# VectorE adds the residual and the LoRA output ahead of the transposed q and copies layer 1's k ahead of the row maxima; ScalarE writes layer 1's high pieces

## The chip, the core and the metric

One Trainium2 chip, one of its cores. The metric is the device time of one execution in microseconds (us), the median of three. The profile's engines are PE (TensorE), DVE (VectorE), ACT (ScalarE), POOL (GpSimd) and SP (SyncE, which issues DMAs only).

## What is computed

Two layers of gated cross attention with a feed-forward part behind each, on x of 8 x 128 tokens by 512 and a context of the same shape. Cut to its core, the reference is:

```python
x = x + tanh(g_xattn[0]) * attn0(layernorm(x), ctx)   # 32 heads of 128, 8 kv heads, RMS norm on q and k
x = x + tanh(g_ffn[0])   * lora(layernorm(x))         # 8 experts of rank 16, a softmax router
x = x + tanh(g_xattn[1]) * attn1(layernorm(x), ctx)   # 16 heads of 96, 4 kv heads, no norm
x = x + tanh(g_ffn[1])   * swiglu(layernorm(x))       # 512 -> 1792 -> 512
# attn: kv = [context, latents]; q, k, v = projections; out = softmax(q k^T / sqrt(hd)) v @ Wo
```

All of it is float32. The kernel gets near that accuracy with pairs: a value is written as a high piece (fp32r, as TensorE reads it) and a low piece (the value less the high one), and each product is three matmuls, high by high, high by low and low by high (`mm3`, L467 to L469).

## The kernel before

There is no scheduler: each engine's program is written out by hand, and semaphores join them. A group is one kv head with its four q heads; layer 0 (`L0`, name "a") has 8 groups, layer 1 (`L1`, name "c") has 4. Within a group a loop runs over the 8 batch elements, so there are 64 + 32 = 96 steps of one tile each. Every engine has its own `step(L, g, b)`, and in it three tiles are under way: the values and the output projection of tile b and of the one before (`prev`), the scores and the softmax of the next (`one`), and the k, v and q projections of the one after (`two`).

TensorE's step is `kv_proj(two)`, `scores(one)`, `q_proj(two)`, `k_turn(two)` (transposes k, L536), `values(b)`, `project(prev)`, `q_turn(two)` (transposes q, L546). Around it the other engines do this:

- ScalarE copies PSUM to SBUF with the high rounding (L706), squares q and k for layer 0's RMS norm (L737, L723), and does the exponentials (`exps`, L760).
- VectorE subtracts for the low pieces (L938), takes the row maxima (`row_max`, L1012), copies layer 1's k (`kv_low`, L988), and adds the projected output to x (`y_add`, L1054).
- The probabilities are divided by their sums and split into a high and a low fp16 piece (`split_probs`: L1029, L1031, high L1036, low L1041). SyncE transposes the pieces by DMA (L426), GpSimd casts them to fp32r (`cast_probs`, L1249), and `values` in the next step reads them. `i` is the half: heads 0 and 1, or 2 and 3.

Three stretches have more in a step than that. In layer 0's first group a layer norm (number 0) stands beside the attention. From the third step of layer 0's last group (L0, g 7) into layer 1's first group, a step also carries the layer norm ahead of the LoRA part (`beside_norm`, number 1), the LoRA part of a tile (`lora`) and the layer norm ahead of layer 1 (`second`, number 2): the tiles run through the seam between the layers one behind the other, and TensorE does `lora_project`, `norm_turn` (L493), `lora_turn` (L607) and `lora_project_out` for them. In layer 1's last group the layer norm ahead of the FFN (number 3) stands beside it. A layer norm is `norm_stats` on VectorE (L950, L952), the reciprocal root on GpSimd (L1218), `norm_scale` on VectorE (L960), `norm_turn` on TensorE, and a high and a low piece on ScalarE and VectorE. `lora_scale` (L1069 to L1073) writes the activations that `lora_turn` transposes; `router_logits` (L1061, L1063) feeds the router's exponential on ScalarE; `lora_add` (L1084) puts the result into x.

The last steps of layer 1 also start the FFN's weights: GpSimd issues their DMAs (L1319, L1320, L1298 and later), among its casts. The FFN then runs by itself to the end.

## Time and profile before

| | |
|---|---|
| median of 3 runs | 1400.72 us (1399.91 to 1400.87) |
| the profiled execution | 1396.48 us, span 1394.4 us |
| PE, DVE, ACT, POOL busy | 94%, 74%, 49%, 36% of the span |
| steps 0 to 95 (both layers) | until 1227 us |
| FFN | 1227 to 1394 us |

Busy time is the union of an engine's instructions; matmuls overlap, and their ends are modelled, so a busy PE is one that has no gap. A step is told by where its `kv_proj` starts on PE: an undisturbed one takes 11.84 us in layer 0 and 10.29 us in layer 1. The granted clock is a share of TensorE's full 2.4 GHz; 0.5 is 1.2 GHz.

### The profile page before, as it was taken

Reading aid. Unit: us, or ns where it says so; the run is one execution under the profiler, and the core shown is the slowest. Engines: PE = TensorE matmul, PEld = TensorE weight load, DVE = VectorE, ACT = ScalarE, POOL = GpSimd, SP = SyncE. Lnnn points to the kernel's source line nnn. Section 1 sums busy time; section 2 is a strip of 40 time slices with the busy share of each in tenths; the row PEclk is TensorE's granted clock in tenths of the full one; section 3 lists DMA queues with packets and bytes.
Section 4 is the critical chain, followed back from the end, with each engine's and each line's share of the span. In section 5 each row is a group of like instructions: output and inputs, shape, how many; then the busy total and the mean of one; then the engine's idle time right before and its main releaser. Section 6 shows DMA issues by size and latency. Waiting matters only on the chain.

```text
span 1394.4 us, 24169 instructions
## 1 busy us (share of the span) xinstructions
PE 1312.8 (94%) x7776; PEld 1150.6 (83%) x7776; DVE 1030.9 (74%) x2620; ACT 680.4 (49%) x2354; POOL 508.2 (36%) x808
## 2 busy tenths in 40 slices
PE   7899999999999999999999888899999998579998
PEld 6788888888888888888887777788888888468887
DVE  5688777777787787777778877888888888533433
ACT  5456665555565566556664433355444543222221
POOL 2445544554455355445544423133223332300000
PEclk8999999999999999999999999999999999789999
DMA  6233332332332332323333211242433322740000
GB/s 189 56 82 76 60 85 62 75 91 46 83 82 46 91 76 61 83 60 73 87 62 68 51 31 31 61 88 58 84 65 72 79 46 47 210 136 1 31 0 31
DMA packets 233439, 98.11 MB, mean 70 GB/s; under 512 B 204800, under 2 KB 217600, under 8 KB 233344
## 3 DMA queue, kind: packets, MB, share of 16 engines
q1 hardware_dynamic: 210416, 58.75, 21.7%
q10 hardware_dynamic: 18992, 27.28, 6.5%
q0 software_dynamic: 3936, 11.01, 2.6%
q8 instruction: 35, 0.57, 0.2%
q14 instruction: 60, 0.49, 0.1%
HBM read 39.08 MB, written 2.10 MB: 30 GB/s over the span
## 4 chain that ended last, share of the span: by engine, by line
PE 71%; DVE 17%; ACT 4%; issue 4%; POOL 2%; DMA 2%; DVEq 0%; SPq 0%; POOLq 0%; ACTq 0%
PE bank L467 18%; PE bank L469 18%; PE bank L468 18%; PE bank L692 7%; DVE split L938 5%; PE bank L678 4%; DVE mx L1012 3%; PE bank L546 3%; DMA turned<-pieces 2%; ACT split L706 2%; DVE pieces L1041 1%; PE bank L536 1%; ACT scratch L760 1%; DVE x L1054 1%; DVE scratch L960 1%
## 5 line engine op out<-in xcount | busy, mean ns | idle before, releaser
L467 PE MATMUL bank<-split 128*128 128x256 f32 (+6 forms) x2120 | 716.7, 338 | 15.5 <-issue 7.2
L469 PE MATMUL bank<-split 128*128 128x256 f32 (+6 forms) x2120 | 696.5, 329 | 0.0
L468 PE MATMUL bank<-split 128*128 128x256 f32 (+6 forms) x2120 | 695.9, 328 | 0.0
L467 PEld LDWEIGHTS bank<-split 128*128 128x128 f32 (+2 forms) x2120 | 405.4, 191 | 48.9 <-issue 10.3
L469 PEld LDWEIGHTS bank<-split 128*128 128x128 f32 (+2 forms) x2120 | 404.6, 191 | 36.4 <-issue 0.2
L468 PEld LDWEIGHTS bank<-split 128*128 128x128 f32 (+2 forms) x2120 | 405.9, 191 | 28.2
L706 ACT ACTIVATE split<-bank 128x512 fp32r<-128x512 f32 (+7 forms) x456 | 194.4, 450 | 325.5 <-PE bank L546 264.0
L1249 POOL CAST split<-turned 128x512 fp32r<-128x512 f16 x384 | 227.9, 622 | 333.9 <-DMA turned<-pieces 333.9
L938 DVE TENSOR_TENSOR split<-bank,split 128x512 fp32r<-128x512 f32 (+7 forms) x456 | 228.0, 503 | 144.0 <-ACT split L706 140.1
L1041 DVE SCALAR_TENSOR_TENSOR pieces<-scratch,rs,pieces 128x256 f16<-128x256 f32 x384 | 180.4, 511 | 0.0
L760 ACT ACTIVATE scratch<-bank,nb,rq 128x256 f32<-128x256 f32 x256 | 141.8, 561 | 63.9 <-DVE nb L1017 63.8
L1012 DVE TENSOR_REDUCE mx<-bank 128x2 f32<-128x512 f32 x192 | 132.1, 688 | 53.4 <-PE bank L469 50.5
L1036 DVE TENSOR_SCALAR pieces<-scratch,rs 128x256 f16<-128x256 f32 x384 | 136.7, 398 | 12.6
L1222 POOL TENSOR_TENSOR split<-raw,split 128x512 fp32r<-128x512 f32 (+1 forms) x90 | 112.4, 1261 | 17.5 <-ACT split L706 16.6
L692 PE MATMUL bank<-split 128*128 128x512 f32 x448 | 107.4, 393 | 0.0
L692 PEld LDWEIGHTS bank<-split 128*128 128x128 f32 x448 | 85.3, 191 | 18.0
L760 ACT ACTIVATE scratch<-bank,nb 128x256 f32<-128x256 f32 x128 | 59.2, 473 | 56.9 <-DVE nb L1020 56.9
L1265 POOL TENSOR_TENSOR qvar<-qsum,hd_eps 128x4 f32<-128x4 f32 x64 | 14.2, 222 | 196.6 <-ACT bank L737 196.6
L723 ACT ACTIVATE scratch<-bank 128x128 f32<-128x128 f32 x128 | 34.3, 274 | 98.5 <-PE bank L469 98.5
L1054 DVE SCALAR_TENSOR_TENSOR x<-bank,tg_attn,x 128x512 f32<-128x512 f32 x96 | 71.0, 740 | 7.1 <-PE bank L469 7.1
L737 ACT ACTIVATE bank<-bank 128x128 f32<-128x128 f32 x256 | 71.3, 284 | 0.0
L706 ACT ACTIVATE split<-raw 128x512 fp32r<-128x512 f32 (+2 forms) x118 | 67.4, 610 | 6.2 <-DMA raw<-in_wkv_a 4.8
(69 smaller groups left out, 1135.3 us busy)
## 6 DMA issues: line engine op xcount, KB each, us to landing
raw<-in_wq_a ACTq DMA_DIRECT2D x14, 512.0 KB, 3.6
raw<-in_wo_a ACTq DMA_DIRECT2D x14, 512.0 KB, 3.4
raw<-in_wkv_a ACTq DMA_DIRECT2D x7, 512.0 KB, 3.4
split<-in_gate_t POOLq DMA_DIRECT2D x2, 1792.0 KB, 7.6
split<-in_up_t POOLq DMA_DIRECT2D x2, 1792.0 KB, 11.2
turned<-pieces SPq DMA_TRANSPOSE x192, 3.1
raw<-in_wq_c ACTq DMA_DIRECT2D x8, 384.0 KB, 3.3
split<-in_down_t POOLq DMA_DIRECT2D x1, 2816.0 KB, 10.6
```

The source lines that it names most:

```text
L467: pe.matmul(out, whi, mhi, start=start, stop=False)
L468: pe.matmul(out, whi, mlo, start=False, stop=False)
L469: return pe.matmul(out, wlo, mhi, start=False, stop=stop)
L692: last = pe.matmul(bank[bk + m % 2][:, :], w[:, k, m * P:(m + 1) * P], part[:, k, toks], start=k == 0 and i == 0, stop=k == KC - 1 and i == 1)
L706: return act.activation(out, in_, ACT.Copy)
L760: act.activation(probs[:, h, :], bank[h // 2][:, (h % 2) * KV:(h % 2 + 1) * KV], ACT.Exp, bias=nb[:, h:h + 1], scale=scale, accum_out=sums ...
L938: return dve.tensor_tensor(out, in_, hi.bitcast(F32), ALU.subtract)
L1012: dve.tensor_reduce(mx[:, pr], chunks(bank[i][:, :], 2), AX.X, ALU.max).then_inc(s.mx_done, 1)
L1036: dve.tensor_scalar(piece[:, i, 0, h, :], probs[:, n, :], rs[:, n:n + 1], None, ALU.mult).then_inc(s.pa_done, 1)
L1041: dve.scalar_tensor_tensor(piece[:, i, 1, h, :], probs[:, n, :], rs[:, n:n + 1], piece[:, i, 0, h, :], ALU.mult, ALU.subtract).then_inc(s. ...
L1222: return pool.tensor_tensor(lo, raw_part, hi.bitcast(F32), ALU.subtract)
L1249: pool.tensor_copy(pT[c].rearrange("p k (h q) -> p h k q", q=P)[:, 2 * i:2 * i + 2], turned_out[:, i, c]).then_inc(s.cast_done[i], 1)
```

## The change

No work is added or taken away but for the source of one operand. Four things move:

- VectorE's order. `y_add` and `lora_add` come ahead of `qt_low` (the low piece of the transposed q); layer 1's `kv_low` comes ahead of `row_max`; `router_logits` comes first, `lora_scale` directly behind `row_max`; the layer norms 0 and 3 are scaled behind `row_max`; the reciprocals of both halves come ahead of the low pieces where ScalarE writes the high ones.
- The high fp16 pieces of layer 1 and of layer 0's last group are written by ScalarE (`probs_high`), two instructions for each half, one ahead of the q copy and one behind the k copy. Elsewhere VectorE still writes them.
- TensorE's `norm_turn` of the layer norms 0 and 3 comes behind `q_proj` and `k_turn`.
- ScalarE squares q from its SBUF copy `qn`, no longer from the PSUM bank, so `q_turn`, which overwrites that bank, no longer waits for the squares.

```diff
+def high_on_scalar(L, g):
+    return L is L1 or is_at(L, g, L0, L0.groups - 1)
# TensorE
             def q_turn(L, g, b):
                 s = attn[L.name]
                 pe.wait_ge(s.qcp_done, count(g, b, 1, 1))
-                if L.normed:
-                    pe.wait_ge(s.qsq_done, count(g, b, NH, NH))
...
-                if beside_norm is not None:
-                    if beside_norm[0] == 1:
-                        wait_prior(pe, *prev, lambda s: s.yadd_done, 1)
+                if beside_norm is not None and beside_norm[0] == 1:
+                    wait_prior(pe, *prev, lambda s: s.yadd_done, 1)
                     norm_turn(*beside_norm)
                 if two is not None:
                     q_proj(*two)
                     k_turn(*two)
+                if beside_norm is not None and beside_norm[0] != 1:
+                    norm_turn(*beside_norm)
# ScalarE
             def q_squares(L, g, b):
...
+                    act.wait_ge(s.qcp_done, count(g, b, 1, 1))
                     for h in range(NH):
-                        act.activation(bank[3][:, h * hd:(h + 1) * hd], bank[6][:, h * hd:(h + 1) * hd], ACT.Square,
+                        act.activation(bank[3][:, h * hd:(h + 1) * hd], qn[:, h * hd:(h + 1) * hd], ACT.Square,
...
+            def probs_high(L, g, b, i):
+                s = attn[L.name]
+                act.wait_ge(s.rs_done, count(g, b, 2, i + 1))
+                wait_prior(act, L, g, b, lambda s: s.turned[i], 16)
+                for h in range(2):
+                    n = 2 * i + h
+                    act.activation(piece[:, i, 0, h, :], probs[:, n, :], ACT.Copy, scale=rs[:, n:n + 1]
+                                   ).then_inc(s.pa_done, 1)
...
+                high = one is not None and high_on_scalar(one[0], one[1])
+                if high:
+                    probs_high(*one, 0)
+                if two is not None:
+                    q_evac(*two)
+                if two is not None:
+                    k_evac(*two)
+                if high:
+                    probs_high(*one, 1)
                 if beside_norm is not None and beside_norm[0] != 1:
                     norm_hi(*beside_norm)
-                if two is not None:
-                    q_evac(*two)
-                    k_evac(*two)
# VectorE: split_probs keeps the sums, the reciprocals and, where high_on_scalar says no,
# the two high pieces; probs_low is what stood behind them
-                for h in range(2):
-                    n = 2 * i + h
-                    dve.tensor_scalar(piece[:, i, 0, h, :], probs[:, n, :], rs[:, n:n + 1], None, ALU.mult
-                                      ).then_inc(s.pa_done, 1)
+                if not high_on_scalar(L, g):
...
+            def probs_low(L, g, b, i):
# VectorE, the order in step(); lines without a sign stay
+                if lora is not None:
+                    router_logits(lora)
                 if second is not None:
                     norm_scale(2, second)
-                if beside_norm is not None:
+                if beside_norm is not None and beside_norm[0] == 1:
                     norm_scale(*beside_norm)
-                if lora is not None:
-                    router_logits(lora)
+                if two is not None and not two[0].normed:
+                    kv_low(*two)
                 if one is not None:
                     row_max(*one, 0)
                     row_max(*one, 1)
-                if two is not None:
+                if lora is not None:
+                    lora_scale(lora)
+                if two is not None and two[0].normed:
                     kv_low(*two)
+                if beside_norm is not None and beside_norm[0] != 1:
+                    norm_scale(*beside_norm)
...
-                if lora is not None:
-                    lora_scale(lora)
                 if one is not None:
                     split_probs(*one, 0)
-                if two is not None:
-                    k_low(*two)
+                    if not high_on_scalar(one[0], one[1]):
+                        probs_low(*one, 0)
+                        if two is not None:
+                            k_low(*two)
+                    split_probs(*one, 1)
...
+                if one is not None:
+                    if high_on_scalar(one[0], one[1]):
+                        probs_low(*one, 0)
+                        if two is not None:
+                            k_low(*two)
+                    probs_low(*one, 1)
...
-                if one is not None:
-                    split_probs(*one, 1)
-                if two is not None:
-                    qt_low(*two)
                 if prev is not None:
                     y_add(*prev)
+                if lora is not None:
+                    lora_add(lora)
+                if two is not None:
+                    qt_low(*two)
                 if next_norm is not None:
                     norm_stats(*next_norm)
                 if lora is not None:
-                    lora_add(lora)
                     norm_stats(2, lora)
                 o_low(L, g, b)
```

The three places where the order moved for the prediction's steps follow, as each program has it; lines have moved by some 5 to 28 between the two files.

On VectorE, in the seam, from `qt_low` (`split` 96x512) at the end of layer 0's last step to the first row maximum (L1012) of layer 1's first step, before:

```order
L938 TENSOR_TENSOR split<-bank,split 96x512
L1054 SCALAR_TENSOR_TENSOR x<-bank,tg_attn,x 128x512
L950 BN_STATS stats<-x 128x6
L952 BN_AGGR moments<-stats 128x2
L1084 SCALAR_TENSOR_TENSOR x<-bank,tg_lora,x 128x512
L950 BN_STATS stats<-x 128x6
L952 BN_AGGR moments<-stats 128x2
L938 TENSOR_TENSOR split<-bank,split 128x512
L960 TENSOR_SCALAR scratch<-x,moments,rstd 128x512 x2
L1061 TENSOR_TENSOR lg<-bank,bias_r 128x8
L1063 TENSOR_REDUCE lmx<-lg 128x1
L1012 TENSOR_REDUCE mx<-bank 128x2
```

The same place with the change, up to where `kv_low` begins (`split` 128x192; the row maxima stand behind it; L1082 is `y_add`, L1112 `lora_add`, L1089 and L1091 `router_logits`, L982 `norm_scale`):

```order
L1082 SCALAR_TENSOR_TENSOR x<-bank,tg_attn,x 128x512
L1112 SCALAR_TENSOR_TENSOR x<-bank,tg_lora,x 128x512
L960 TENSOR_TENSOR split<-bank,split 96x512
L972 BN_STATS stats<-x 128x6
L974 BN_AGGR moments<-stats 128x2
L972 BN_STATS stats<-x 128x6
L974 BN_AGGR moments<-stats 128x2
L960 TENSOR_TENSOR split<-bank,split 128x512
L1089 TENSOR_TENSOR lg<-bank,bias_r 128x8
L1091 TENSOR_REDUCE lmx<-lg 128x1
L982 TENSOR_SCALAR scratch<-x,moments,rstd 128x512 x2
L960 TENSOR_TENSOR split<-bank,split 128x192
```

Both additions now stand ahead of the low piece of q, the router's logits ahead of the scaling, and layer 1's `kv_low` ahead of the maxima.

On ScalarE, in the first step of layer 1 (still in the seam), from the router's exponential (L802) to the transposed q (`split` 96x512), before:

```order
L802 ACTIVATE lg,lsum<-lg,lmx 128x8
L760 ACTIVATE scratch,sums<-bank,nb 128x256 x2
L706 ACTIVATE split<-bank 128x4x128 x2
L760 ACTIVATE scratch,sums<-bank,nb 128x256 x2
L706 ACTIVATE scratch<-bank 128x384
L706 ACTIVATE split<-bank 96x256
L706 ACTIVATE split<-bank 128x128
L706 ACTIVATE split<-bank 96x512
```

The same step with the change (L818 is the router's exponential, L765 the exponentials of the softmax, L777 `probs_high`, L710 the copies):

```order
L818 ACTIVATE lg,lsum<-lg,lmx 128x8
L765 ACTIVATE scratch,sums<-bank,nb 128x256 x2
L710 ACTIVATE split<-bank 128x4x128 x2
L765 ACTIVATE scratch,sums<-bank,nb 128x256 x2
L777 ACTIVATE pieces<-scratch,rs 128x256 x2
L710 ACTIVATE scratch<-bank 128x384
L710 ACTIVATE split<-bank 96x256
L777 ACTIVATE pieces<-scratch,rs 128x256 x2
L710 ACTIVATE split<-bank 128x128
L710 ACTIVATE split<-bank 96x512
```

The two pairs of high pieces stand ahead of the q copy and behind the k copy; the LoRA activations' high piece (128x128) and q's come behind them.

On TensorE, in the third step of layer 1's last group, from the last matmul of the scores into `q_proj` (128x384), before (L493 is `norm_turn` of layer norm 3):

```order
L469 MATMUL bank<-split 128x256
L493 MATMUL bank<-ident,scratch 128x128 x4
L467 MATMUL bank<-split 128x384
L468 MATMUL bank<-split 128x384
L469 MATMUL bank<-split 128x384
L467 MATMUL bank<-split 128x384
```

With the change, from the end of `q_proj` to the first matmuls of the values (96x512; L498 is `norm_turn`, L541 `k_turn`):

```order
L474 MATMUL bank<-split 128x384
L472 MATMUL bank<-split 128x384
L473 MATMUL bank<-split 128x384
L474 MATMUL bank<-split 128x384
L541 MATMUL bank<-ident,scratch 96x128 x2
L498 MATMUL bank<-ident,scratch 128x128 x4
L472 MATMUL bank<-split 96x512
L473 MATMUL bank<-split 96x512
L474 MATMUL bank<-split 96x512
```

The transposes of the layer norm moved from ahead of the 12 matmuls of `q_proj` to behind the transposes of k.

## Rows read from the trace of the kernel before

**Rows 1.** the page: busy us, share of the span, instructions by engine
```profile
PE 1312.8 (94%) x7776; PEld 1150.6 (83%) x7776; DVE 1030.9 (74%) x2620; ACT 680.4 (49%) x2354; POOL 508.2 (36%) x808
```

**Rows 2.** busy time (count) by engine and stage, clock, DMA share, GB/s
```profile
0.00:103.31 103.31, 87.90 (x509) 77.55 (x509) 73.23 (x186) 54.50 (x191) 39.90 (x77) 0.93 0.43 110
103.31:737.25 633.94, 630.33 (x3819) 555.43 (x3817) 490.35 (x1232) 374.50 (x1397) 311.44 (x482) 1.00 0.33 71
737.25:906.05 168.80, 145.96 (x906) 127.90 (x905) 135.70 (x365) 68.57 (x236) 54.67 (x96) 0.97 0.24 50
906.05:1143.00 236.95, 230.33 (x1540) 209.01 (x1538) 203.79 (x580) 118.53 (x384) 77.65 (x111) 1.00 0.36 72
1143.00:1227.00 84.00, 61.38 (x336) 52.19 (x335) 60.92 (x163) 26.20 (x87) 22.67 (x42) 0.85 0.50 130
```

**Rows 3.** TensorE's waits, 0 to 103 us: total, times, longest
```profile
PE bank L493 <- DVE scratch L960: 6.4, 5, 3.2
PE bank L546 <- ACT bank L737: 5.7, 3, 2.2
```

**Rows 4.** TensorE's waits, 737 to 906 us
```profile
PE bank L607 <- DVE scratch L1073: 11.3, 8, 2.4
PE bank L467 <- issue: 5.8, 6, 1.0
PE bank L493 <- DVE scratch L960: 5.0, 6, 2.0
```

**Rows 5.** four of the ten steps of that stretch, each a window
```profile
765.91:783.64 17.73, 15.61 (x100) 13.48 (x98) 13.88 (x38) 7.88 (x30) 7.03 (x14) 1.00 0.26 55
...
839.51:857.18 17.67, 14.72 (x100) 12.96 (x97) 13.72 (x38) 5.61 (x18) 4.21 (x9) 1.00 0.16 31
857.18:876.66 19.48, 15.72 (x97) 13.65 (x94) 16.88 (x41) 7.98 (x24) 7.19 (x10) 0.91 0.13 25
...
891.80:906.05 14.25, 12.24 (x76) 11.21 (x74) 11.74 (x31) 5.28 (x17) 3.08 (x6) 0.88 0.29 66
```

**Rows 6.** VectorE's timeline in the step from 839.51 us
```profile
840.42 0.69 DVE L938 TENSOR_TENSOR split<-bank,split 96x512 fp32r<-96x512 f32 x1 [2.42 <-ACT split L706]
841.02 0.74 DVE L1054 SCALAR_TENSOR_TENSOR x<-bank,tg_attn,x 128x512 f32<-128x512 f32 x1
...
842.62 0.72 DVE L1084 SCALAR_TENSOR_TENSOR x<-bank,tg_lora,x 128x512 f32<-128x512 f32 x1
...
847.02 0.15 DVE L1061 TENSOR_TENSOR lg<-bank,bias_r 128x8 f32<-128x8 f32 x1
```

**Rows 7.** TensorE's waits, 906 to 1143 us
```profile
PE bank L536 <- DVE scratch L988: 4.8, 6, 1.1
```

**Rows 8.** ScalarE's timeline in a step of layer 1, its longest wait
```profile
1066.22 1.85 ACT L706 ACTIVATE split<-bank 96x512 fp32r<-96x512 f32 x5 [3.29 <-PE bank L546]
```

**Rows 9.** casts of GpSimd in the same step
```profile
1059.14 1.17 POOL L1249 CAST split<-turned 128x512 fp32r<-128x512 f16 x2 [0.94 <-DMA turned<-pieces]
```

**Rows 10.** TensorE's timeline in the same step, the transposes of k
```profile
1061.94 0.38 PE L536 MATMUL bank<-ident,scratch 128*96 128x128 f32 x2
```

**Rows 11.** TensorE's waits, 1143 to 1227 us
```profile
PE bank L493 <- DVE scratch L960: 18.2, 6, 10.9
```

**Rows 12.** TensorE's timeline, the first of four equal waits in that stretch
```profile
1146.51 0.66 PE L493 MATMUL bank<-ident,scratch 128*128 128x128 f32 x4 [1.26 <-DVE scratch L960]
```

**Rows 13.** GpSimd's timeline, 1186 to 1232 us
```profile
1194.93 1.03 POOL L1319 DMA_DIRECT2D split<-in_gate_t  x1
...
1210.20 1.17 POOL L1249 CAST split<-turned 128x512 fp32r<-128x512 f16 x2 [12.73 <-DMA turned<-pieces]
```

**Rows 14.** groups of instructions: count, busy us, mean ns, idle before
```profile
L1036 DVE TENSOR_SCALAR pieces<-scratch,rs 128x256 f16<-128x256 f32 x384 | 136.7, 398 | 12.6
...
L737 ACT ACTIVATE bank<-bank 128x128 f32<-128x128 f32 x256 | 71.3, 284 | 0.0
...
L746 ACT ACTIVATE split<-bank,qkw 128x256 fp32r<-128x256 f32 x64 | 30.7, 479 | 0.0
```

19 lines of the change are left out of this document (14 added, 5 removed).

## The prediction

> **What bounds the kernel now.** I read the page first, then the busy time by stage, then TensorE's waits stage by stage, then single steps. The page has TensorE busy for 94% of the span [rows 1]. The stages show how that 94% is spread [rows 2]: from 103 to 737 us TensorE has 3.6 us of gaps in 633.9, at full clock. No other engine can give anything there, however early it is. What is left lies in four stretches: the start (15.4 us of gaps), the seam between the layers (168.8 less 146.0, so 22.8), the rest of layer 1 (6.6) and its last group with the way to the FFN (22.6). The clock is below 1.00 in the start, the seam and the last group, the stretches with the gaps. So the question is which of these waits the change ends, and what is late next.
>
> **The seam, ten steps.** Three waits hold 22.1 of the 22.8 us [rows 4]: `lora_turn` waits 11.3 us for `lora_scale`, `lora_project` 5.8 us (put down to issue; by the code it waits for `lora_add` of the tile before), `norm_turn` 5.0 us for `norm_scale`.
>
> VectorE's timeline shows why [rows 6]. It idles 2.42 us until ScalarE has q's high piece, takes `qt_low`, and only then `y_add` (0.74) and `lora_add` (0.72), though `project`, which `y_add` needs, ended ahead of `q_turn`. With the change `y_add` lies in that idle time and `lora_add` needs only the LoRA matmuls. `lora_project` loses its wait, and the two statistics, the root on GpSimd and `norm_scale` all come some 1.46 us earlier (0.74 + 0.72). That covers the `norm_turn` waits but for the layer norm's last step. `router_logits`, at 847.02 in the row, no longer waits for the scaling, and `lora_scale` leaves its place behind two low pieces, a gain near their 2 x 0.69.
>
> What is late next: with these waits gone, `values` waits for the low piece of layer norm 2, which VectorE reaches behind `kv_low`, the maxima and `lora_scale`, about 0.5 us after TensorE is ready. In the steps behind one of layer 1, whose `o_low` has four parts, I add 0.4 to 0.9 us. A second new lateness is ScalarE's: `lora_act_hi` and, while `two` is of layer 0, `q_squares` now stand behind four more instructions.
>
> I lay each step out by the rows' durations: TensorE's busy time less the part that only refills after a wait, plus what is late. Of those shown [rows 5]: 17.73 becomes 15.3, 17.67 becomes 15.0, 19.48 becomes 15.9 and 14.25 becomes 12.2. The other six, in order, go from 13.7 to 13.1, 14.9 to 14.6, 18.3 to 16.0, 19.9 to 16.0, 17.7 to 15.0 and 15.1 to 13.5. Together 168.8 becomes 146.6, which is 22.2 less. Of that 4.0 us are the clock: its share of 0.91 in a step of 19.48 is 1.75 us, and three steps have such a dip. Whether fewer gaps keep the clock up no row can say; I take half of it. **Seam: 20 us**, between 9 (each remaining wait twice as long as I think) and 23.
>
> **What ScalarE's new work costs.** Four high pieces a step for 40 tiles. VectorE takes 398 ns for one [rows 14], and loses all four. ScalarE's nearest row is the k copy of layer 0, same 128x256 with a pointer for scale, 479 ns [rows 14]; but it reads PSUM and writes fp32r. So 4 x 0.48 = 1.9 us a step, overlaps ignored; the bounds are the square's 284 ns at half the width (1.1 us) and 2.4 us, were it a quarter dearer than the k copy. In a step of layer 1 its longest wait is 3.29 us, ahead of q's transposed copy [rows 8]. 1.9 fits with 1.4 to spare, so I cost it at nothing; without that cover it would be 0.5 to 1 us a step. In the seam's steps with layer 0's squares it is not covered: that is the lateness above.
>
> The Trainium skill speaks against this move: in "ScalarE: Activation LUTs", section "Rules for kernel authors", a multiply belongs on VectorE, and the section "What ACT_TABLE_LOAD costs" gives 186 ns plus 93 for a pointer operand plus 0.833 ns a column. By that a piece would be about 0.49 us as an estimate and four of them 2.0 us against VectorE's 1.6; the row of the k copy agrees to 0.01. What the rule leaves out is which engine is waited for, and by it the move would cost the sum 0.4 us a step or 16 us in all if ScalarE were on the path. The page of "VectorE: DVE Perf Modes", section "The TRN2 errata", also has ScalarE reading SBUF dearer than PSUM (224 against 172 cycles at 1.2 GHz, an estimate of 43 ns more for a square from `qn`); no row here shows that price.
>
> The squares' new source costs nothing in layer 0's full stretch, as ScalarE is busy for 374.5 of 633.9 us there [rows 2].
>
> **The rest of layer 1, 906 to 1143 us.** `k_turn` waits six times, 4.8 us, for the copy of k [rows 7]. With `kv_low` ahead of the maxima and some 1.6 us less on VectorE a step, these end; each also costs TensorE some 0.2 to 0.3 us of refilling. **6.5 us**, bounds 4.8 and 8.4 (8.4 if the one wait for GpSimd's weight piece goes too). The maxima come 0.35 to 0.7 us later for it. Covered: the piece's casts are done at 1060.31 [rows 9], and TensorE reaches `values` behind `k_turn` at about 1062.1 [rows 10], 1.8 us later; and the second half's low pieces come out 0.5 to 0.7 us earlier than now, since the chain no longer runs through all of half 0 first.
>
> **The last group.** `norm_turn` of layer norm 3 waits 1.26 us in each of four steps [rows 12]. Moved behind `q_proj` (2.3 us) and `k_turn` it would have no wait, but `norm_scale` now also stands behind the maxima: I find 0.4 us of wait left, **3.6 us** gained for the four. In the next step, which has no q to project, `norm_turn` comes 1.3 us later than now. That is hidden: from 1194.93 the FFN's weights hold the DMA queues, and GpSimd gets the last tile's transposed pieces only at 1210.20 after 12.73 us of waiting [rows 13]. The end of this stretch hangs on when those weights are issued, behind a cast whose pieces come earlier: **0.9 us**. The 10.9 us wait stays [rows 11].
>
> **The start.** `q_turn` waits three times, 5.7 us, for the squares [rows 3], and `norm_turn` five times, 6.4 us. The first is removed but ScalarE still squares ahead of copying q back, so only the transposes' 0.7 us move out of the chain each time where that copy is waited for. The second gives way to `k_turn`, which needs the root that GpSimd computes behind a cast waiting for its DMA. By hand: 2.6 us from the first step, 2.4 from the next three. **5 us**, bounds 3 and 8.
>
> Layer 0's full stretch: `y_add` first lets `o_low` and the weights' low pieces come 0.7 us earlier at the steps that change groups, worth at most its 3.6 us of gaps. **0.5 us.** Where VectorE has no idle time, `y_add` instead pushes `qt_low` back by 0.7; `scores` has 3.1 us of `kv_proj` ahead of it.
>
> **Sum.** 20 + 6.5 + 3.6 + 0.9 + 5 + 0.5 = 36.5 us. The profiled execution took 1396.48 us (span 1394.4), which becomes 1360.0; it lay 4.2 us under the median of the runs, so the median of 1400.72 becomes **1364 us**.
>
> **Rivals.**
> - *ScalarE is late in the seam and at the start.* The high pieces, with the low ones on VectorE waiting for them, push `lora_act_hi`, q's copies and so `lora_add` back; the waits move instead of ending. For it: VectorE and ScalarE now hand each other four pieces a step, and the seam's steps have the longest chains. Against it: ScalarE is busy for 68.6 of 168.8 us there [rows 2]. The seam would give 9 instead of 20, the start 3 instead of 5, the last group nothing: 1400.7 - 9 - 6.5 - 3 - 1 = about 1381 us. Chance 0.26.
> - *The moves do little.* Every wait for VectorE is replaced by one about as long behind the next of its pieces, since its work is the same and only layer 1's k copy is truly ahead of need: 6.5 us and some of the start, 1392 us. Against it: VectorE has 33 us of idle time in the seam [rows 2]. Chance 0.08.
> - *Slower.* The pieces of each tile in layer 1 and layer 0's last group reach the transposing DMA later, and `values` waits for the casts. The margin is 1.8 us, about 2.4 with the earlier second half. The gain over these 40 steps is near 36/40 = 0.9 us a step, so it turns once the pieces come 3.3 us later than I find; at 4 us later the price is 40 x 1.6 = 64 us, or about 1428. The skill's rule on multiplies points this way; by the rows two exchanges between engines would have to cost 3 us. Chance 0.04.
> - *The forecast*, 1354 to 1373 by its own bounds. Chance 0.62.
>
> The range of 8 in 10 takes the forecast's and most of the first rival: 1354 to 1385. A measurement here tells 0.2%, 2.8 us. Within it: 0.02, between the second rival and the last. Faster by more 0.94, slower by more 0.04.
>
> **What the new profile would show.** Right: the seam's ten steps in about 149 us, no wait of `lora_project` for `lora_add`, `lora_turn`'s waits under 3 us in sum; no wait of `k_turn` for the copy of k behind 906 us; four waits of `norm_turn` under 0.6 us in the last group; steps of 10.29 us in layer 1 with ScalarE's wait ahead of q down to about 1.4 us. Wrong: `values` waiting for casts, a new wait of `lora_project_out` for its low piece over 1 us a step, or a step of layer 1 above 10.29 us that was not so before.

## The result and the profile after

The changed kernel took 1357.72 us, the median of 6 runs (1354.71 to 1358.87), against 1400.23 us (1397.24 to 1400.87, 6 runs) before: a ratio of 0.9697, 95% interval 0.9683 to 0.9711, 3.0% faster. The forecast was 1364, range 1354 to 1385. The profiled execution after took 1356.93 us, with a span of 1355.1 us. Of the runs below, one of e3 at 1847.05 us with a granted clock of 0.65 and one of the kernel before at 2741.38 us stand far off all others and are left out of the medians and ratios.

The page of the changed kernel, busy time by engine, answers to [rows 1]:

```profile
PE 1300.6 (96%) x7776; PEld 1140.5 (84%) x7776; DVE 992.5 (73%) x2464; ACT 744.2 (55%) x2510; POOL 507.5 (37%) x808
```

156 instructions went from VectorE to ScalarE, four for each of 39 tiles: layer 1's 32 and the last seven of layer 0's last group (the program reaches the group's first tile out of its loop, where `high_on_scalar` says no). ScalarE's load rose by 64 us and VectorE's fell by 38. TensorE does the same 7776 matmuls in 12 us less busy time; 6.3 of them are in the seam, where its idle time fell and its clock rose (below).

The stages of the changed kernel, columns as in [rows 2], cut at the same steps:

```profile
0.00:98.07 98.07, 85.25 (x509) 74.59 (x509) 73.37 (x187) 55.29 (x191) 39.42 (x77) 0.97 0.47 116
98.07:732.74 634.67, 630.54 (x3820) 555.46 (x3818) 492.09 (x1226) 379.67 (x1405) 312.19 (x482) 1.00 0.32 72
732.74:880.08 147.34, 139.62 (x906) 123.36 (x904) 122.91 (x322) 84.96 (x276) 53.94 (x96) 1.00 0.29 55
880.08:1111.00 230.92, 230.40 (x1540) 209.02 (x1538) 183.73 (x493) 151.91 (x472) 76.53 (x109) 1.00 0.37 74
1111.00:1187.55 76.55, 57.81 (x336) 49.57 (x335) 53.47 (x142) 34.26 (x107) 23.51 (x43) 0.90 0.59 143
```

The start gained 5.2 us, layer 0's full stretch lost 0.7, the seam gained 21.5, the rest of layer 1 6.0, and the last group with the way to the FFN 7.5. That is 39.5 of the 39.55 us between the two profiled executions. The seam's clock is 1.00 where it was 0.97, with 7.7 us of gaps where there were 22.8.

TensorE's waits in the seam, after (total, times, longest), against [rows 4]:

```profile
PE bank L472 <- DVE split L960: 4.5, 7, 1.4
PE bank L498 <- DVE scratch L982: 2.4, 4, 1.0
PE bank L541 <- DVE scratch L1007: 0.3, 1, 0.3
PE bank L610 <- DVE scratch L1101: 0.2, 1, 0.2
```

The waits of `lora_turn` fell from 11.3 to 0.2 us (L610), those of `lora_project` are gone, and `norm_turn` (L498) halved. New is L472 waiting for a low piece (L960, the function `low`): the low piece of layer norm 2 that `values` waits for, 0.3 to 0.7 us in six steps, and once the low piece that `lora_project_out` needs:

```profile
852.59 0.50 PE L472 MATMUL bank<-split 128*128 128x512 f32 x1 [1.38 <-DVE split L960]
```

The four steps that answer to [rows 5]:

```profile
759.52:774.57 15.05, 15.05 (x99) 13.33 (x98) 12.70 (x35) 9.53 (x34) 5.73 (x13) 1.00 0.28 59
...
821.36:836.18 14.82, 14.34 (x100) 12.86 (x97) 12.60 (x35) 7.22 (x22) 4.05 (x8) 1.00 0.19 36
836.18:853.74 17.56, 14.40 (x97) 12.25 (x94) 15.77 (x38) 9.58 (x28) 8.02 (x11) 1.00 0.16 30
867.59:880.08 12.49, 11.18 (x76) 9.89 (x74) 10.06 (x27) 6.86 (x21) 3.09 (x6) 1.00 0.28 69
```

By hand they were to be 15.3, 15.0, 15.9 and 12.2. Three agree to 0.3 us. The third, 17.56, does not, and is taken up below.

VectorE's timeline at the start of the step from 821.36 us, against [rows 6] (`y_add` L1082, `lora_add` L1112, `qt_low` L960 96x512, `router_logits` L1089, the last part of `lora_scale` L1101):

```profile
820.53 0.75 DVE L1082 SCALAR_TENSOR_TENSOR x<-bank,tg_attn,x 128x512 f32<-128x512 f32 x1 [0.43 <-PE bank L474]
821.21 0.75 DVE L1112 SCALAR_TENSOR_TENSOR x<-bank,tg_lora,x 128x512 f32<-128x512 f32 x1
822.27 0.69 DVE L960 TENSOR_TENSOR split<-bank,split 96x512 fp32r<-96x512 f32 x1 [0.31 <-ACT split L710]
...
825.62 0.17 DVE L1089 TENSOR_TENSOR lg<-bank,bias_r 128x8 f32<-128x8 f32 x1 [0.48 <-PE bank L474]
...
829.79 0.29 DVE L1101 TENSOR_TENSOR scratch<-bank,lg 128x128 f32<-128x128 f32 x1
```

The wait ahead of `qt_low` is 0.31 us where it was 2.42: both additions now lie in it, and both are over before the next step's `kv_proj` is a microsecond old. `router_logits` now waits 0.48 us for TensorE's LoRA projection, where it stood behind the scaling before.

In a step of layer 1, ScalarE ahead of q's transposed copy (against [rows 8]), and the two groups that answer to [rows 14] (count, busy, mean ns, idle before):

```profile
1036.43 1.85 ACT L710 ACTIVATE split<-bank 96x512 fp32r<-96x512 f32 x5 [1.19 <-PE bank L549]
```

```profile
L742 ACT ACTIVATE bank<-scratch 128x128 f32<-128x128 f32 x256 | 72.6, 286 | 0.0
L777 ACT ACTIVATE pieces<-scratch,rs 128x256 f16<-128x256 f32 x156 | 70.9, 511 | 3.4 <-DVE rs L1053 3.1
```

A high piece takes ScalarE 511 ns (0.92 us for two that overlap), and the wait fell from 3.29 to 1.19 us.

### The profile page after: what moved, and what is told of

Its sections match the earlier page's. It is cut to its first block, busy times and chain, and to the rows that moved or that the text cites. A ratio compares the mean times of both kernels' runs of the same rounds, so it can differ in the third digit from the quotient of the medians.

```text
span 1355.1 us, 24187 instructions
## 1 busy us (share of the span) xinstructions
PE 1300.6 (96%) x7776; PEld 1140.5 (84%) x7776; DVE 992.5 (73%) x2464; ACT 744.2 (55%) x2510; POOL 507.5 (37%) x808
## 4 chain that ended last, share of the span: by engine, by line
PE 72%; DVE 13%; ACT 5%; issue 4%; POOL 3%; DMA 3%; DVEq 0%; ACTq 0%; POOLq 0%
PE bank L472 19%; PE bank L474 19%; PE bank L473 18%; PE bank L696 8%; DVE split L960 4%; PE bank L682 4%; PE bank L549 2%; DVE mx L1034 2%; DMA turned<-pieces 2%; ACT split L710 2%; DVE pieces L1069 2%; ACT scratch L765 1%; PE bank L541 1%; POOL split L1264 1%; DVE scratch L1007 1%
## 5 line engine op out<-in xcount | busy, mean ns | idle before, releaser
L472 PE MATMUL bank<-split 128*128 128x256 f32 (+6 forms) x2120 | 711.7, 336 | 14.9 <-DVE split L960 11.0
L472 PEld LDWEIGHTS bank<-split 128*128 128x128 f32 (+2 forms) x2120 | 402.2, 190 | 50.4 <-DVE split L960 12.3
L710 ACT ACTIVATE split<-bank 128x512 fp32r<-128x512 f32 (+7 forms) x456 | 194.1, 449 | 231.3 <-PE bank L549 172.6
L960 DVE TENSOR_TENSOR split<-bank,split 128x512 fp32r<-128x512 f32 (+7 forms) x456 | 224.6, 504 | 54.1 <-ACT split L710 46.8
L765 ACT ACTIVATE scratch<-bank,nb,rq 128x256 f32<-128x256 f32 x256 | 141.8, 561 | 59.4 <-DVE nb L1039 59.4
L1264 POOL TENSOR_TENSOR split<-raw,split 128x512 fp32r<-128x512 f32 (+1 forms) x90 | 113.7, 1274 | 22.2 <-ACT split L710 22.2
L1082 DVE SCALAR_TENSOR_TENSOR x<-bank,tg_attn,x 128x512 f32<-128x512 f32 x96 | 71.8, 748 | 49.2 <-PE bank L474 49.0
L765 ACT ACTIVATE scratch<-bank,nb 128x256 f32<-128x256 f32 x128 | 59.2, 473 | 69.2 <-DVE nb L1042 69.2
L1059 DVE TENSOR_SCALAR pieces<-scratch,rs 128x256 f16<-128x256 f32 x228 | 85.7, 418 | 8.4
L777 ACT ACTIVATE pieces<-scratch,rs 128x256 f16<-128x256 f32 x156 | 70.9, 511 | 3.4 <-DVE rs L1053 3.1
L742 ACT ACTIVATE bank<-scratch 128x128 f32<-128x128 f32 x256 | 72.6, 286 | 0.0
## 6 DMA issues: line engine op xcount, KB each, us to landing
split<-in_up_t POOLq DMA_DIRECT2D x2, 1792.0 KB, 11.2
```

Source lines behind the costliest of these rows:

```text
L472: pe.matmul(out, whi, mhi, start=start, stop=False)
L710: return act.activation(out, in_, ACT.Copy)
L765: act.activation(probs[:, h, :], bank[h // 2][:, (h % 2) * KV:(h % 2 + 1) * KV], ACT.Exp, bias=nb[:, h:h + 1], scale=scale, accum_out=sums ...
L960: return dve.tensor_tensor(out, in_, hi.bitcast(F32), ALU.subtract)
L1059: dve.tensor_scalar(piece[:, i, 0, h, :], probs[:, n, :], rs[:, n:n + 1], None, ALU.mult).then_inc(s.pa_done, 1)
L1264: return pool.tensor_tensor(lo, raw_part, hi.bitcast(F32), ALU.subtract)
```

## The experiments

All are the changed kernel with one edit, but for the second, which is nearer to the kernel before. Each was timed in turn with the kernel before, five times (e2 twelve times, e3 six), and the ratios are to those runs of the kernel before. The table has the median, and from each profiled execution the stages, told by where a step's `kv_proj` starts: the start, layer 0's full stretch, the ten steps of the seam, the rest of layer 1, the last group's four steps, and from there to the end.

```text
kernel            median    start  layer 0  seam   rest L1  last 4  to the end
before           1400.23    103.3   633.9   168.8   234.8    50.5    203.0
changed          1357.72     98.1   634.7   147.3   228.8    45.6    200.7
e1 order only    1360.08     95.8   633.8   153.5   228.5    46.2    200.3
e2 pieces only   1399.73    105.7   634.6   167.7   236.1    50.1    200.0
e3 y_add late    1374.51     97.0   634.1   159.0   230.2    48.4    204.0
e4 k copy late   1362.07     96.8   635.6   145.8   235.7    45.3    202.7
e5 lora late     1370.26     97.3   635.6   160.1   231.7    45.7    200.3
e6 norm early    1374.81    109.0   634.7   147.4   228.8    52.2    198.5
e7 squares PSUM  1357.00    100.1   634.5   146.7   231.4    45.3    199.3
e8 late FFN      1351.61     98.0   634.6   147.5   232.0    45.7    193.9
e9 pieces all    1359.21    100.8   633.0   147.3   231.3    45.8    199.9
e10 scalar 4     1360.51     97.2   635.2   147.5   230.9    46.0    201.9
e11 scalar 8     1378.61     97.7   634.9   147.4   246.7    49.0    201.9
e12 combined     1351.39     97.7   635.1   145.7   229.0    45.7    196.4
```

Where the code is the same, the seam repeats to 0.2 us and the last four steps to 0.5. But the start varies from 95.8 to 100.8 us, layer 0 by 2, the rest of layer 1 from 228.8 to 232.0 (mostly whether TensorE waits for GpSimd's weight piece, 1.6 to 1.9 us in some executions and not at all in others), and the last column by 3 to 4. A stage is evidence beyond that only.

**Order or relief (e1 and e2).** The two halves of the change apart. e1:

```diff
 def high_on_scalar(L, g):
-    return L is L1 or is_at(L, g, L0, L0.groups - 1)
+    return False
```

> The changed kernel, but VectorE writes all high pieces again (high_on_scalar says no everywhere); all other moves stay. If the order makes the gain, most of the 42.5 us stay: VectorE has 24 us of idle time in the seam and needs 1.6 us a step more (40 steps), of which the layer norm 2's low piece, the LoRA scaling and the k copy all stand ahead of the pieces. I expect the seam near 152 us, the rest of layer 1 without waits of k_turn, and 1364 us, between 1360 and 1370. If the relief of VectorE makes the gain, waits of k_turn and norm_turn come back and the time is 1380 us or more.

e2, the pieces on ScalarE and the old places of nearly all else:

```diff
+                high = one is not None and high_on_scalar(one[0], one[1])
+                if high:
+                    probs_high(*one, 0)
...
# y_add, lora_scale, router_logits, kv_low, norm_turn and the squares as before
```

> The other half alone: ScalarE writes the high pieces of layer 1 and of layer 0's last group, with the reciprocals of both halves ahead of the low pieces, and everything else (y_add, lora_add, lora_scale, router_logits, layer 1's k copy, norm_turn, the squares' source) stands as in the kernel before. By the order theory it gains little: the waits of lora_turn, lora_project and k_turn keep their causes, each 0 to 1.6 us shorter; 1392 us, between 1385 and 1400. By the relief theory it gains most of the 42.5 us: 1375 us or less.

e1 measured a ratio of 0.9732 (0.9709 to 0.9755) to the kernel before, 1360.08 us, e2 1.0004 (0.9990 to 1.0018), 1399.73 us, at the upper end of its range. The order alone makes nearly all of the gain; the pieces alone make none. TensorE's waits in e2, in the seam and behind it:

```profile
PE bank L612 <- DVE scratch L1102: 11.3, 8, 2.4
PE bank L498 <- DVE scratch L983: 8.3, 15, 2.0
PE bank L541 <- DVE scratch L1011: 0.9, 1, 0.9
...
PE bank L541 <- DVE scratch L1011: 7.0, 8, 1.5
```

The first three lines are the seam, the last is the rest of layer 1. `lora_turn` waits the same 11.3 us in eight steps as in [rows 4], although VectorE is idle for 45 of 167.7 us instead of 33 of 168.8. `k_turn` waits 7.0 us where it waited 4.8 [rows 7].

e2 isn't the pieces alone to the last line: `lora_add` stands behind `y_add` and ahead of the next tile's statistics, where the kernel before had it behind them, and the low pieces of the layer norms 0 and 3 stand behind the second half's pieces. The first shows: `lora_project` waits only 0.1 us a step for `lora_add`, where it waited 0.8 to 1.0 [rows 4], and `norm_turn` waits 8.3 us instead of 5.0. The seam as a whole gained 1.1 us by all of it.

In the seam of e1, `values` and `lora_project_out` wait more for low pieces than in the changed kernel, 7.0 us against 4.5:

```profile
PE bank L472 <- DVE split L960: 7.0, 12, 1.9
```

So the pieces are worth 6.1 us of the seam once the order is there, and nothing in the rest of layer 1 (228.5 and 228.8). In the ratios they are about 5 us (0.0035 of 1400), but the two intervals touch at 0.971, so the seam shows the gain better than the whole time does.

**The residual and the LoRA output (e3).**

```diff
+                if two is not None:
+                    qt_low(*two)
                 if prev is not None:
                     y_add(*prev)
                 if lora is not None:
                     lora_add(lora)
-                if two is not None:
-                    qt_low(*two)
```

> The changed kernel with y_add and lora_add behind qt_low again. Theory: lora_project waits for lora_add again and the norms come 1.46 us later in ten steps; the seam goes from 147.3 to 155 to 161 us, the rest is unchanged: 1368 us, between 1364 and 1373. Rival, that ScalarE's pieces gave VectorE the room: at most 3 us are lost, 1361 us or less.

Measured 0.9817 (0.9788 to 0.9846), 1374.51 us: the theory's side, and 1.5 us beyond its range. The seam is 11.6 us longer, as expected. What I left out is the last group, 2.8 us longer, where layer norm 3 hangs on `y_add` too. TensorE's waits for the layer norms in the seam and in the last group:

```profile
PE bank L498 <- DVE scratch L982: 8.7, 14, 2.0
...
PE bank L498 <- DVE scratch L982: 3.0, 4, 0.8
```

One part of the expectation did not come: `lora_project` waits only 0.1 us a step, although `lora_add` stands behind `qt_low` again. It still stands ahead of the next tile's statistics, as in e2. So the 0.8 to 1.0 us that `lora_project` waited before were for the statistics ahead of `lora_add`, and `y_add` behind `qt_low` costs its time at `norm_turn`: 8.7 us where the changed kernel has 2.4.

**Layer 1's k copy (e4).**

```diff
-                if two is not None and not two[0].normed:
-                    kv_low(*two)
                 if one is not None:
                     row_max(*one, 0)
                     row_max(*one, 1)
+                if two is not None and not two[0].normed:
+                    kv_low(*two)
```

> The changed kernel with layer 1's kv_low behind row_max again. Theory: k_turn waits about six times behind the seam and once or twice in it, 5 to 6 us: 1363 us, between 1361 and 1366. Rival, that the 1.6 us a step taken off VectorE end these waits by themselves: 1358 to 1359 us, no wait of k_turn over 0.2 us.

Measured 0.9730 (0.9711 to 0.9750), 1362.07 us, as expected. Behind the seam `k_turn` waits again, more than in [rows 7], with VectorE's relief in place:

```profile
PE bank L541 <- DVE scratch L1010: 6.6, 7, 1.5
```

In the seam the late copy is better by 1.5 us: `values` and `lora_project_out` wait 2.2 us for low pieces instead of 4.5. The copy ahead of the maxima makes them 0.6 us later, and with them ScalarE's exponentials and the high piece of layer norm 2 that stands behind these; VectorE's low piece follows it. In the step from 821.36 us it starts 4.30 us behind the start of `norm_scale`, in the same step of e4 4.09.

**The LoRA scaling (e5).** `router_logits` behind the norms' scaling and `lora_scale` behind their low pieces:

```diff
-                if lora is not None:
-                    router_logits(lora)
...
+                if lora is not None:
+                    router_logits(lora)
...
-                if lora is not None:
-                    lora_scale(lora)
...
                     norm_low(*beside_norm)
+                if lora is not None:
+                    lora_scale(lora)
```

> The changed kernel with router_logits behind the layer norms' scaling and lora_scale behind their low pieces again. Theory: lora_turn waits again some 1 us in eight steps, so the seam is 8 to 11 us longer than 147.3 us: 1367 us, between 1363 and 1370. Rival, that y_add and lora_add ahead of qt_low have made room enough: at most 3 us lost, 1361 us or less.

Measured 0.9783 (0.9765 to 0.9800), 1370.26 us, 0.3 us above the range; the seam is 12.7 us longer, where I expected 8 to 11, with a clock of 0.97. `lora_turn` waits more than in the kernel before:

```profile
PE bank L610 <- DVE scratch L1101: 13.7, 7, 3.5
```

**The layer norms 0 and 3 (e6).**

```diff
-                if beside_norm is not None and beside_norm[0] == 1:
-                    wait_prior(pe, *prev, lambda s: s.yadd_done, 1)
+                if beside_norm is not None:
+                    if beside_norm[0] == 1:
+                        wait_prior(pe, *prev, lambda s: s.yadd_done, 1)
                     norm_turn(*beside_norm)
# norm_scale ahead of row_max, norm_hi ahead of q's copy; norm_low stays behind probs_low
```

> The changed kernel with the layer norms 0 and 3 scaled, turned and copied where they stood before. Theory: norm_turn waits 0.9 to 1.3 us again in each of the last group's four steps and two or three times in the start; the last group loses 4 us, the start 2 to 3: 1363.5 us, between 1361 and 1366. Rival, that the earlier y_add alone ends these waits: 1359 us or less.

Measured 0.9826 (0.9805 to 0.9846), 1374.81 us. The direction is the theory's, the size is not: 17 us lost instead of 6. The start, at 109.0 us, is 11 us longer, outside all that the same code shows, and longer than before the change; the last group's steps lose 6.6. TensorE's waits for the norms in the start, 6.4 us in [rows 3]:

```profile
PE bank L498 <- DVE scratch L981: 11.8, 6, 4.0
```

The kernel before had a shorter way behind the early `norm_turn`: `norm_low` stood ahead of the second half's pieces. The change moved it behind them, and this edit leaves it there. That can be part of it only: e2 has the same early `norm_turn` with the same late `norm_low`, and its start took 105.7 us, with 7.5 us of these waits. The other 3.3 us to 109.0 come with what e6 has beside that in the start, `y_add` ahead of `qt_low` and the squares' new source, or with the start's own variation; no run tells these apart.

**The squares (e7).**

```diff
                 pe.wait_ge(s.qcp_done, count(g, b, 1, 1))
+                if L.normed:
+                    pe.wait_ge(s.qsq_done, count(g, b, NH, NH))
...
-                        act.activation(bank[3][...], qn[...], ACT.Square,
+                        act.activation(bank[3][...], bank[6][...], ACT.Square,
```

> The changed kernel with ScalarE squaring q from PSUM and q_turn waiting for the squares again. Theory: only the start and, in the seam, the two steps that still square q for layer 0 notice it, 0.7 to 2.6 us: 1359.5 us, between 1358 and 1361. Rival, that the squares' source is what shortened the start: the start loses its whole 5 us, 1363 us.

Measured 0.9692 (0.9675 to 0.9709), 1357.00 us: 1 us below the range, and no difference from the changed kernel. The profile has `q_turn` waiting 4.8 us for the squares again. Its first full step ends at 34.1 us, where the nine profiles with the new source and the same start have 31.8 to 33.5; but its start of 100.1 us lies within what the same code shows. Over the whole kernel, what this part brings can't be told from nothing.

**The FFN's weights (e8).** The first DMAs of the FFN are issued one step later:

```diff
-                if is_at(L, g, L1, L1.groups - 1) and b == NT - 2:
+                if is_at(L, g, L1, L1.groups - 1) and b == NT - 1:
```

> The changed kernel, but GpSimd issues the FFN's first weights one step later, behind the last tile's casts. Theory: the 11.4 us wait of norm_turn near 1175 us is the last tile's transposed pieces behind those weights in the DMA queues, so it shrinks to 2 to 3 us; gate and up (3.6 MB at the 0.41 MB per us of the page) then need 9 us from about 1166 on, about when the FFN could start: 8 us gained, 1350 us, between 1347 and 1354. Rival, that the wait moves to the FFN's first matmul: 1357 us or more.

Measured 0.9659 (0.9637 to 0.9681), 1351.61 us, 6 us less than the changed kernel and inside the range. In the changed kernel the weights are issued at 1157.22 us, and GpSimd then waits for the last tile's pieces:

```profile
1157.22 1.03 POOL L1361 DMA_DIRECT2D split<-in_gate_t  x1
1172.93 1.17 POOL L1291 CAST split<-turned 128x512 fp32r<-128x512 f16 x2 [13.12 <-DMA turned<-pieces]
```

TensorE's wait behind it, at 1175.86 us:

```profile
1175.86 1.11 PE L498 MATMUL bank<-ident,scratch 128*128 128x128 f32 x4 [11.39 <-DVE scratch L982]
```

With the late issue the same cast waits 6.84 us and the same `norm_turn` 4.16:

```profile
1167.42 1.18 POOL L1291 CAST split<-turned 128x512 fp32r<-128x512 f16 x2 [6.84 <-DMA turned<-pieces]
```

```profile
1172.29 0.66 PE L498 MATMUL bank<-ident,scratch 128*128 128x128 f32 x4 [4.16 <-DVE scratch L982]
...
1184.25 3.90 PE L696 MATMUL bank<-split 128*128 128x512 f32 x16 [0.91 <-DMA split<-in_up_t]
```

The wait that is left is above the 2 to 3 us that I expected. The FFN then waits 0.91 us for its weights, so a still later issue can be expected to cost there what it gives here; none was run. By the timeline the 4.16 us that stay are the chain from `project` over `y_add`, the statistics and the root to the scaling.

**How much ScalarE can still take (e9 to e11).** e9 gives it the high pieces of layer 0 too, all but its first group's:

```diff
-    return L is L1 or is_at(L, g, L0, L0.groups - 1)
+    return not is_at(L, g, L0, 0)
```

> The changed kernel with ScalarE writing the high pieces in layer 0 too, all but its first group: 1.8 us a step more on ScalarE and 1.2 us less on VectorE for some 48 tiles more. Theory: TensorE waits for neither there, ScalarE goes from 60% to about 75% busy and the stretch stays at 634 to 636 us: 1358 us, between 1356 and 1361. Rival, that a piece on ScalarE costs its place in the chain (squares, q's transposed copy and the next maxima late): 0.5 us a step or more, 1380 us.

Measured 0.9709 (0.9689 to 0.9729), 1359.21 us, the theory's time. ScalarE is busy for 457.9 us of layer 0's stretch of 633.0 instead of 379.7 of 634.7, and TensorE notices nothing. e10 and e11 add work that nobody reads ahead of q's transposed copy, four and eight squares:

```diff
                     q_squares(*two)
+                    if L is L1:
+                        act.wait_ge(attn[L1.name].qcp_done, count(two[1], two[2], 1, 1))
+                        for h in range(4):   # e11: range(8)
+                            act.activation(bank[3][:, h * 48:(h + 1) * 48], qn[:, h * 48:(h + 1) * 48],
+                                           ACT.Square, accum_out=qsum[:, h:h + 1])
```

> The changed kernel with four more squares of 48 columns on ScalarE ahead of q's transposed copy in 30 steps of layer 1, some 0.9 us a step at 0.22 us each (an estimate from the 0.29 us that four squares of 128 columns are apart in layer 0); nobody reads them. ScalarE waits 1.19 us there, so nothing is lost: 1358 us, between 1356 and 1360. Rival, that the pieces have already used the cover up: 0.9 us a step, 1385 us.

> The same with eight such squares, some 1.8 us a step and 0.6 us over the cover. Theory: q's low piece comes 0.6 us later and scores has about 0.7 us to spare behind kv_proj, so at most 0.2 us a step are lost: 1361 us, between 1357 and 1365. Rival, that all over the cover is lost: 0.6 us in 30 steps, 1376 us; and if none of it was covered, 54 us.

e10: 0.9721 (0.9701 to 0.9741), 1360.51 us, 0.5 us above its range, with an interval that overlaps that of the changed kernel. e11: 0.9851 (0.9834 to 0.9868), 1378.61 us. In e10 the undisturbed steps stay at 10.29 us. In nine steps the copy still waits, mostly 0.28 us; where the rounding of the next group's weights had already used part of the wait, it starts straight behind the last square. Only the step with most of that rounding grows, by 0.6 to 0.8 us three times:

```profile
943.53 0.21 ACT L887 ACTIVATE bank<-scratch 128x48 f32<-128x48 f32 x1
943.66 0.21 ACT L887 ACTIVATION_READ_ACCUMULATOR bank<-scratch 128x1 f32 x1
943.75 1.84 ACT L710 ACTIVATE split<-bank 96x512 fp32r<-96x512 f32 x5
```

In e11 TensorE waits in nearly every step ahead of `scores`, for q's low piece, mostly 0.2 to 0.6 us and three times 1.3 to 1.4:

```profile
950.97 0.38 PE L472 MATMUL bank<-split 96*128 96x256 f32 x1 [0.61 <-DVE split L965]
```

The squares are 0.22 us apart, so eight are 1.8 us, 0.6 more than the wait of 1.19. The plain steps went from 10.29 to between 10.6 and 11.2 us, and the three with most rounding lost 1.8 to 2.5 us each, 21 us in all, 0.7 a step. So the rival's size was right: all that is over the cover is lost.

But not because `scores` has nothing to spare. In e10 the copy starts 1.08 us into the step at 912.18 us, 0.8 later than in an undisturbed step, and that step takes 10.31 us like the same one of the changed kernel. What the squares lengthen is a ring of ScalarE and VectorE that doesn't pass through TensorE: q's transposed copy, the output's high pieces behind it, their low pieces on VectorE, layer 1's k copy and the maxima behind them, then the exponentials, the pieces and the next copy. In e11, VectorE and then ScalarE (L965 is `low`, L1039 the maxima):

```profile
972.86 1.90 DVE L965 TENSOR_TENSOR split<-bank,split 96x384 fp32r<-96x384 f32 x5 [0.56 <-ACT split L710]
...
975.01 0.68 DVE L1039 TENSOR_REDUCE mx<-bank 128x2 f32<-128x512 f32 x1
```

```profile
981.78 1.85 ACT L710 ACTIVATE split<-bank 96x512 fp32r<-96x512 f32 x5
```

The copy before that one started at 970.99 us. The ring is 10.79 us long, and so is the step; in the changed kernel it is 10.29 with 1.19 us of waiting in it. The maxima there start 4.3 us into a step, in e11 5.6.

**Combined (e12).** e8, and the k copy late only where the LoRA part stands in the step:

```diff
+                beside_lora = lora is not None or second is not None
-                if two is not None and not two[0].normed:
+                if two is not None and not two[0].normed and not beside_lora:
                     kv_low(*two)
# row_max(*one, 0), row_max(*one, 1)
+                if two is not None and not two[0].normed and beside_lora:
+                    kv_low(*two)
```

> The late issue of the FFN's weights and layer 1's k copy behind the maxima where the LoRA part or layer norm 2 stands in the step, ahead of them elsewhere. The first gave 6 us, the second 1.5 us in the seam without the 6.9 us that it cost behind it: 1350 us, between 1347 and 1352. Rival, that the gain in the seam was chance: 1351.6 us as with the late issue alone.

Measured 0.9656 (0.9639 to 0.9673), 1351.39 us, inside the range. It beats both kernels, but not e8 by anything that can be told. In its profile the seam is 145.7 us as in e4, 1.6 less than in the changed kernel; the medians don't bear it out, and they don't speak against it.

## Why the prediction was right, step by step

- **Seam: 20 forecast, 21.5 came.** The mechanism was the forecast's in the main: e3 and e5 give 11.6 and 12.7 us of it back, one by one. Together that is more than the whole; that a late `y_add` and a late `lora_scale` delay the same chain is an argument, as no run has both late and all else early. One cause was misread: what kept `lora_project` waiting was the statistics ahead of `lora_add`, not `qt_low` (e2 and e3 have `qt_low` first and 0.1 us of wait). The change moved both, so the sum didn't suffer. The layout said 22.2 with 4.0 us of clock in it, and I took half of the clock. By the clocks of the three steps with a dip (0.91 in those from 801.93 and 857.18 us, 0.88 in that from 891.80), they come to 5.3 us by the same reckoning and not 4.0. All of it came back: 1.00 in the seam, 0.99 in e1 with 10.9 us of gaps, 0.97 in e5 with 16.2.
- **The step forecast at 15.9 took 17.56.** This is the one place where a term of a step was wrong, and one of the signs named as "wrong" showed there: `lora_project_out` waits 1.38 us for its low piece. In the nine others the layout by hand is within 0.9 us, and all ten add up to 147.3 against 146.6. VectorE lost time to GpSimd in it (below).
- **ScalarE's new work: 1.9 us a step, hidden, 1.4 left.** It was 1.84, and 1.19 left. e10 and e11 show that the cover was about as thick as the row said and no thicker, if for another reason than `scores` (above). VectorE's own saving was over-sized: I took 398 ns a piece from the group's mean, while two take 0.62 us in a step of layer 1, so a step saves 1.2 us and not 1.6. The Trainium skill's rule ("ScalarE: Activation LUTs", section "Rules for kernel authors") that a multiply belongs on VectorE speaks against the move. Per piece the rows agree with it (511 ns on ScalarE, 351 on VectorE with no weight subtraction beside it), for the whole they don't: the move was worth 6 us of the seam (e1), as VectorE was waited for and ScalarE not.
- **Rest of layer 1: 6.5 forecast, 6.0 came** between the two profiles; over the seven profiles of the same code the mean is 230.4 us, a gain of 4.4, under the lower bound of 4.8. No `k_turn` waits. The difference is the wait for GpSimd's weight piece, 0 to 1.9 us, which I had only put at the upper bound: it was there before (1.8 us) and happened to be absent in the profile after, and that is luck. e4 puts the gain on the place of the k copy; the relief of VectorE, which I named beside it, has no share (e1, e2).
- **Last group: 3.6 forecast, 4.9 came** in four steps (from 12.2 to 10.9). I had left 0.4 us of wait in each; the profile has 0.22 us once. The maxima ahead of `norm_scale` delay it less than I found.
- **The way to the FFN: 0.9 forecast, 2.3 came.** That is within the 4 us by which this stage varies. The long wait stayed, 11.39 us for 10.9 [rows 11]. The cause that I gave for it, the FFN's weights ahead of the last tile's pieces in the DMA queues, is borne out by e8: with the later issue it falls to 4.16.
- **Start: 5 forecast, 5.2 came.** The split of it, 2.6 us for the squares and `norm_turn` in the first step and 2.4 in the next three, came in place but not by cause: the first full step ends 2.6 us earlier than before (32.1 for 34.7 us) and the next ones give the rest, but e7 shows no gain for the squares in the time, and e6 shows 11 us for the norms' new places. And the nine profiles of the new start spread over 5 us (mean 97.7), so the direction is shown, its exact size is not.
- **Layer 0's full stretch: 0.5 forecast, a loss of 0.7 came**, inside the 2 us by which it varies. The term should have been nothing.
- **Sum: 36.5 forecast, 39.55 came** between the profiled executions; that the terms, each off by up to 2 us, came out 3 us apart in sum is luck in part. The other 3.4 us of the distance to the median of 1357.72 are the starting point: I carried over that the profiled execution lay 4.2 us under the median, and after it lay only 0.8 under.

The rival on ScalarE failed because TensorE waits for none of the pieces, and VectorE for 4.0 us of them in all. "The moves do little" is refuted by e1, and the slower case by the profile: no `values` waits for a cast in the seam or in layer 1's full stretch.

## What to carry to other kernels

When one engine's waits all name the same other engine, look first for what that engine does ahead of the piece that is waited for, and only then at how busy it is: here 156 instructions less on VectorE were worth nothing alone, and the same instructions in another order were worth 38 us (e1's ratio); relief pays afterwards, in the stretch with the longest chain only. A cover is used up once: a wait of 3.29 us hid 1.84 us of work and 0.9 more, and 1.8 more cost all that was over. To know how thick it is, follow the ring of engines that comes back to the instruction behind the wait; the slack of the engine that reads its result next can be larger and doesn't help.

## What the runs showed of the hardware

**VectorE beside GpSimd.** In the step of 17.56 us two scalings take 2.38 us and a multiply of two columns 1.16 us (usually 0.16). VectorE and GpSimd in the changed kernel, the same stretch:

```profile
841.09 2.38 DVE L982 TENSOR_SCALAR scratch<-x,moments,rstd 128x512 f32<-128x512 f32 x2
...
848.00 1.16 DVE L1051 TENSOR_SCALAR sums_in<-sums 128x2 f32<-128x2 f32 x1
```

```profile
841.16 1.27 POOL L1264 TENSOR_TENSOR split<-raw,split 128x512 fp32r<-128x512 f32 x1
842.38 1.55 POOL L1291 CAST split<-turned 128x512 fp32r<-128x512 f16 x2
...
847.84 1.29 POOL L1264 TENSOR_TENSOR split<-raw,split 128x512 fp32r<-128x512 f32 x1 [2.65 <-ACT split L710]
```

Each VectorE line's instructions can be sorted by what GpSimd does meanwhile. The scaling takes 544 ns without either of them (16 times), 761 beside a cast (15, from 534 to 947) and 1627 beside a weight subtraction (once, with a cast as well). The high piece in the kernel before took 351 ns without and 919 beside a subtraction (32 times, eight of them not slowed, 1387 at most), which is how its mean came to 398 [rows 14]. The maxima, which read PSUM, take 688, 685 and 679 ns: they notice nothing. The spread of one line, as min/median/max ns, for the scaling, then for the maxima of the changed kernel:

```profile
L982 DVE TENSOR_SCALAR scratch<-x,moments,rstd x32: 531/547/1627, 7.0 to 1193.8; 128x512 f32<-128x512 f32 x32
```

```profile
L1034 DVE TENSOR_REDUCE mx<-bank x192: 673/690/693, 22.4 to 1157.4; 128x2 f32<-128x512 f32 x192
```

The Trainium skill's page "GPSIMD Engine Reference", section "1. Specifications", says that GpSimd shares its SBUF interfaces with VectorE, with contention for VectorE instructions in a two-port mode or with two SBUF inputs. The rows fit that, though none names an instruction's mode: what is slowed goes from SBUF to SBUF, though not all that does is slowed (a two-column reciprocal takes 166 ns either way), and what reads PSUM isn't. They add the price: up to four times for the high piece, three for the scaling, and the two-column multiply lasts nearly as long as the subtraction beside it. So the mean of a group is no good duration for a step in which GpSimd is idle, nor for one in which it isn't.

**The squares' source.** A square from SBUF takes 286 ns, from PSUM 284 [rows 14]. By the Trainium skill, "VectorE: DVE Perf Modes", section "The TRN2 errata", it would be some 43 ns more (224 against 172 cycles at 1.2 GHz, an estimate); this case doesn't show that.
